# Reordered copies in a four-layer attention and expert kernel: a copy ahead of a normalisation, output spreading on VectorE, half-word reads of rounded values

## The reference

```python
x = x + L0_xattn(ln(x), ctx)   # 8 heads of 64: softmax(q k' / 8) v, projection, bias
x = x + L0_ffn(ln(x))          # 16 heads of 64 with rope and causal mask, then 31 experts of which 3 count, one shared
x = x + L1_xattn(ln(x), ctx)   # 16 heads of 8, key mask
x = x + L1_ffn(ln(x))          # 16 heads of 8 on 4 key heads, rope, causal; then 8 gated experts of which 2 count
x = x + L2_xattn(ln(x), ctx)   # linear in x plus a mean over ctx
x = x + L2_ffn(ln(x))          # 32 gated experts of which 4 count, with a capacity
x = x + L3_xattn(ln(x), ctx)   # one head of 128, two kinds of position
x = x + L3_ffn(ln(x))          # the quantised gated layer below
# L3_ffn, with act_qdq(t) = clip(round(t / s), -32768, 32767) * s,  s = max(|t|) / 32767 over the whole tensor
x = act_qdq(x)
up = act_qdq(x @ dequant(w_up).T)
gate = act_qdq(x @ dequant(w_gate).T)
sig = clip(round(sigmoid(gate) * 65536), 0, 65535) / 65536
gate = act_qdq(gate * sig)
o = act_qdq(gate * up)
return o @ dequant(w_down).T
```

## Time and profile before

| what | value |
|---|---|
| runs (3) | median 1324.61 us, 1323.27 to 1331.30 |
| profiled execution, own time | 1321.66 us |
| its span, first to last instruction | 1319.8 us, mean granted TensorE clock 0.961 |
| busy: PE / PEld / DVE / ACT / POOL | 88% / 68% / 75% / 66% / 42% |
| chain that ended last, by engine | PE 59%, ACT 17%, DVE 14%, issue 7% |
| steps of l0x, without POOL beside them | 7.97 us |
| steps of l0f | 14.54 us |
| steps of l1x | 8.18 us |
| steps of l1f | 8.34 us |
| l3m, from the end of DVE's first scale of the gate (1252.94) to the join of the six maxima (1284.87) | 31.9 us |

### The profile page before, as it was taken

The page is one execution under the profiler, slowest core; times in us unless marked ns, Lnnn a source line. Parts: engine busy times, 40 slices in busy tenths (PEclk is TensorE's granted clock), DMA queues, the critical chain, the costliest instruction groups (busy, mean ns, idle before and its releaser), DMA issues.

```text
span 1319.8 us, 29320 instructions
## 1 busy us (share of the span) xinstructions
PE 1160.2 (88%) x10082; PEld 894.7 (68%) x10082; DVE 995.9 (75%) x2234; ACT 875.7 (66%) x2403; POOL 560.5 (42%) x670
## 2 busy tenths in 40 slices
PE   7889889999988999997888899988999989997815
PEld 4677777788766788885666677766788666666403
DVE  6676677667758899997777766767666787887787
ACT  4666466656654799995888777764566447775684
POOL 5710366766653222255222231132877417881100
PEclk8999999999998999997999999998999899998967
DMA  5230000000002556650000010003222028750001
GB/s 168 60 93 16 20 2 2 2 3 2 2 2 87 181 210 212 209 208 1 2 2 2 3 42 2 2 2 114 88 88 84 0 55 206 190 139 1 1 0 33
DMA packets 38865, 83.71 MB, mean 63 GB/s; under 512 B 6066, under 2 KB 19762, under 8 KB 38740
## 3 DMA queue, kind: packets, MB, share of 16 engines
q1 hardware_dynamic: 38740, 82.07, 20.2%
HBM read 80.40 MB, written 1.64 MB: 62 GB/s over the span
## 4 chain that ended last, share of the span: by engine, by line
PE 59%; ACT 17%; DVE 14%; issue 7%; POOL 2%; DMA 1%; ACTq 0%; SPq 0%; POOLq 0%; DVEq 0%
PE score_bank L1662 18%; ACT h_all L1096 13%; PE f_bank L1696 6%; PE score_bank L1521 6%; PE f_bank L1422 4%; PE turn_bank L1537 4%; PE turn_bank L1696 3%; PE out_bank L1696 3%; PE out_bank L1577 2%; PE out_bank L1546 2%; DVE top_score L2006 2%; PE f_bank L1447 1%; DVE work L2018 1%; PE f_bank L1454 1%; DVE part_max L2404 1%
## 5 line engine op out<-in xcount | busy, mean ns | idle before, releaser
L1096 ACT ACTIVATE h_all<-score_bank,top_score 128x128 f32<-128x128 f32 x896 | 276.6, 400 | 101.3 <-DVE top_score L2006 101.2
L1662 PE MATMUL score_bank<-parts 128*128 128x512 f32 x1040 | 296.4, 403 | 9.8 <-DVE h_parts L2212 6.6
L1662 PEld LDWEIGHTS score_bank<-parts 128*128 128x128 f32 x1040 | 191.9, 190 | 75.2 <-DVE h_parts L2212 19.0
L2006 DVE TENSOR_REDUCE top_score<-score_bank 128x4 f32<-128x512 f32 x224 | 143.1, 681 | 105.2 <-PE score_bank L1521 105.2
L2212 DVE TENSOR_TENSOR h_parts<-score_bank,h_parts 128x512 fp32r<-128x512 f32 x260 | 178.3, 686 | 2.7 <-ACT h_parts L1211 2.4
L1211 ACT ACTIVATE h_parts<-score_bank 128x512 fp32r<-128x512 f32 x260 | 155.5, 598 | 31.8 <-PE f_bank L1696 8.5
L778 POOL TENSOR_TENSOR small<-small,half_neg 128x4 f32<-128x4 f32 (+4 forms) x24 | 36.6, 1528 | 177.0 <-DVE small L1981 83.2
L1537 PE MATMUL turn_bank<-CF,h_all 128*128 128x128 f32 x512 | 81.7, 283 | 30.3 <-DVE work L2018 19.0
L1537 PEld LDWEIGHTS turn_bank<-CF,h_all 128*128 128x128 f32 x512 | 56.1, 142 | 57.1 <-POOL h_all L803 18.1
L1188 ACT ACTIVATE score_bank<-score_bank,wset 128x512 f32<-128x512 f32 x128 | 84.6, 662 | 11.8 <-PE score_bank L1662 7.0
L2184 DVE TENSOR_TENSOR score_bank<-work,score_bank 128x512 f32<-128x512 f32 x124 | 86.3, 696 | 8.2 <-ACT score_bank L1188 5.6
(11 more groups left out here) (417 smaller groups left out, 2623.6 us busy)
## 6 DMA issues: line engine op xcount, KB each, us to landing
work<-gates_l0m SPq DMA_DIRECT2D x62, 512.0 KB, 3.9
W0X<-gates_l2m SPq DMA_DIRECT2D x32, 256.0 KB, 3.9
CTX<-gates_l2m SPq DMA_DIRECT2D x32, 256.0 KB, 3.9
wset<-in_l0m SPq DMA_DIRECT2D x32, 128.5 KB, 3.6
W0X<-gates_l1m SPq DMA_DIRECT2D x8, 512.0 KB, 3.8
wset<-in_l1m SPq DMA_DIRECT2D x8, 384.0 KB, 4.6
CTX<-gates_l1m SPq DMA_DIRECT2D x6, 512.0 KB, 4.0
big<-in_w0f SPq DMA_DIRECT2D x4, 512.0 KB, 3.9
```

Source lines behind the costliest of these rows:

```text
L1096: last = act.activation(held[c][:, P * m:P * m + P], score_bank[c][:, P * m:P * m + P], ACT.Exp, bias=top_score[c][:, m:m + 1], **sums)
L1662: last = pe_.matmul(bk[:, :], wt, y[:, x], start=(part == 0), stop=(part == len(parts_of) - 1))
L2006: dve.tensor_reduce(top_score[c][:, :], split(score_bank[c][:, :], HEADS), AX_X, ALU.max, negate=True)\
```

## The change

1. l0x: on DVE, C 0 of the batch before stands ahead of N 0 of the own batch.
2. l1x and l1f: SP is DVE's, behind M 3, with the same waits and the same signal; OB comes behind C 1 on DVE and behind T 1 on PE. In l1x C 2 goes from DVE to ACT, behind OT.
3. The matmul of two columns ahead of the causal mask is dropped (l0f and l1f).
4. l3m: `gate_steps` and `other` are dropped. The sigmoid and the products read the low 16 bits of the rounded float as an int16, with a step of two (`steps_in`). A one-column Sigmoid stands ahead of the wait for the first scale. Copies and chunk maxima come in another order, three of U's roundings after the wait for the third scale, three among the last roundings of the gate.
5. POOL's wait at the first two batches of l1f names the use of the front bank by l1x's own count of fronts (4) rather than l1f's (3).

```diff
@@ -54,4 +55,4 @@
              ("F", 3, "next")],
-        DVE=[("M", 0, "own"), ("M", 1, "own"), ("CS", 0, "next"), ("OP", 0, "before"), ("N", 0, "own"), ("C", 0, "last"), ("C", 1, "last"),
-             ("N", 1, "own"), ("Y", 0, "after")],
+        DVE=[("M", 0, "own"), ("M", 1, "own"), ("CS", 0, "next"), ("OP", 0, "before"), ("C", 0, "last"), ("N", 0, "own"),
+             ("C", 1, "last"), ("N", 1, "own"), ("Y", 0, "after")],
         POOL=[]),
@@ -70,8 +71,8 @@
         PE=[("S", 0, "own"), ("OP", 0, "before"), ("F", 1, "next"), ("V", 0, "last"), ("V", 1, "last"), ("V", 2, "last"),
-            ("V", 3, "last"), ("F", 2, "next"), ("T", 0, "own"), ("OB", 0, "last"), ("T", 1, "own"), ("F", 3, "next"),
+            ("V", 3, "last"), ("F", 2, "next"), ("T", 0, "own"), ("T", 1, "own"), ("OB", 0, "last"), ("F", 3, "next"),
             ("F", 0, "after"), ("T", 2, "own"), ("OT", 0, "last"), ("T", 3, "own")],
-        ACT=[("F", 0, "next"), ("E", 0, "own"), ("SP", 0, "last"), ("E", 1, "own"), ("F", 1, "next"), ("E", 2, "own"),
-             ("E", 3, "own"), ("F", 3, "next"), ("OT", 0, "last"), ("C", 3, "own")],
-        DVE=[("M", 0, "own"), ("OP", 0, "before"), ("M", 1, "own"), ("M", 2, "own"), ("M", 3, "own"), ("F", 2, "next"),
-             ("C", 0, "own"), ("OB", 0, "last"), ("C", 1, "own"), ("C", 2, "own")],
+        ACT=[("F", 0, "next"), ("E", 0, "own"), ("E", 1, "own"), ("F", 1, "next"), ("E", 2, "own"),
+             ("E", 3, "own"), ("F", 3, "next"), ("OT", 0, "last"), ("C", 2, "own"), ("C", 3, "own")],
+        DVE=[("M", 0, "own"), ("OP", 0, "before"), ("M", 1, "own"), ("M", 2, "own"), ("M", 3, "own"), ("SP", 0, "last"), ("F", 2, "next"),
+             ("C", 0, "own"), ("C", 1, "own"), ("OB", 0, "last")],
         POOL=[("Y", 0, "after")]),
@@ -79,8 +80,8 @@
         PE=[("S", 0, "own"), ("OP", 0, "before"), ("F", 1, "next"), ("V", 0, "last"), ("V", 1, "last"), ("V", 2, "last"),
-            ("V", 3, "last"), ("F", 2, "next"), ("T", 0, "own"), ("OB", 0, "last"), ("T", 1, "own"),
+            ("V", 3, "last"), ("F", 2, "next"), ("T", 0, "own"), ("T", 1, "own"), ("OB", 0, "last"),
             ("F", 0, "after"), ("T", 2, "own"), ("OT", 0, "last"), ("T", 3, "own")],
-        ACT=[("F", 0, "next"), ("E", 0, "own"), ("SP", 0, "last"), ("E", 1, "own"), ("E", 2, "own"), ("E", 3, "own"),
+        ACT=[("F", 0, "next"), ("E", 0, "own"), ("E", 1, "own"), ("E", 2, "own"), ("E", 3, "own"),
              ("C", 2, "own"), ("OT", 0, "last"), ("C", 3, "own")],
-        DVE=[("M", 0, "own"), ("OP", 0, "before"), ("M", 1, "own"), ("M", 2, "own"), ("M", 3, "own"), ("F", 1, "next"),
-             ("C", 0, "own"), ("OB", 0, "last"), ("F", 2, "next"), ("C", 1, "own")],
+        DVE=[("M", 0, "own"), ("OP", 0, "before"), ("M", 1, "own"), ("M", 2, "own"), ("M", 3, "own"), ("SP", 0, "last"), ("F", 1, "next"),
+             ("C", 0, "own"), ("C", 1, "own"), ("OB", 0, "last"), ("F", 2, "next")],
         POOL=[("Y", 0, "after")]),
@@ -328,2 +328,7 @@
 
+        def steps_in(t, at):
+
+            h = HIDDEN_ORDER[at]
+            return t[:, 1024 * h:1024 * h + 1024].bitcast(I16).rearrange("p (n two) -> p n two", two=2)[:, :, 0]
+
 
@@ -823,3 +828,3 @@
 
-                                r, k = place(front_at["l1x"], L["front"], PAIRS - 1, s, 0)
+                                r, k = place(front_at["l1x"], LAYERS[2]["front"], PAIRS - 1, s, 0)
                                 pool.wait_ge(f_drained[r], k + 1)
@@ -1104,7 +1108,2 @@
                             .then_inc(copied if L["dim"] == 64 else copied_by["ACT"], 1)
-                    if what == "SP":
-
-                        act.wait_ge(weighed, unit_no(L, i, s, 0) + 8)
-                        act.wait_ge(regrouped, narrow_no(L, i, s) + 1)
-                        act.activation(spread_o[:, :], out_bank[:, :], ACT.Copy).then_inc(gathered, 1)
                     if what == "OT":
@@ -1334,2 +1333,4 @@
 
+            act.activation(prob_rec[0][:, 0:1], top_score[0][:, 0:1], ACT.Sigmoid)
+
             act.wait_ge(step("l3m.scale"), 1)
@@ -1358,11 +1359,6 @@
             def sigmoid(at):
-                act.wait_ge(step("l3m.g"), at + 1)
+                act.wait_ge(step("l3m.g_round"), at + 1)
                 if at >= 2:
                     act.wait_ge(step("l3m.gs"), at - 1)
-                act.activation(sig[at % 2][:, :], piece(big, at), ACT.Sigmoid, scale=quant[:, 2, 2:3]).then_inc(step("l3m.sig"), 1)
-
-            def other(at):
-
-                act.wait_ge(step("l3m.u_round"), at + 1)
-                act.activation(piece(U, at), piece(U, at), ACT.Identity, bias=less_magic[:, :]).then_inc(step("l3m.u"), 1)
+                act.activation(sig[at % 2][:, :], steps_in(big, at), ACT.Sigmoid, scale=quant[:, 2, 2:3]).then_inc(step("l3m.sig"), 1)
 
@@ -1374,13 +1370,8 @@
                 rounded(big, at, 2, "l3m.g_round")
-                if at < 3:
-                    copies(0, at + 1)
-                if at == 4:
-                    act.wait_ge(step("l3m.scale"), 3)
-                if at >= 4:
-                    rounded(U, at - 4, 1, "l3m.u_round")
+                if 0 < at < 4:
+                    copies(0, at)
                 sigmoid(at)
-            for at in range(2, 6):
+            act.wait_ge(step("l3m.scale"), 3)
+            for at in range(3):
                 rounded(U, at, 1, "l3m.u_round")
-            for at in range(2):
-                other(at)
             act.wait_ge(step("l3m.scale"), 4)
@@ -1388,4 +1379,4 @@
                 rounded(big, at, 3, "l3m.round3")
-                if 1 <= at <= 4:
-                    other(at + 1)
+                if at < 3:
+                    rounded(U, at + 3, 1, "l3m.u_round")
             act.wait_ge(step("l3m.scale"), 5)
@@ -1497,4 +1488,2 @@
 
-                            pe_.matmul(banks[0][:, 0:2], ident_bf, own_bf[:, 0:2], start=True, stop=True, skip_group_check=True)
-
                             for j in range(4):
@@ -2019,2 +2008,7 @@
                             .then_inc(copied if L["dim"] == 64 else copied_by["DVE"], 1)
+                    if what == "SP":
+
+                        dve.wait_ge(weighed, unit_no(L, i, s, 0) + 8)
+                        dve.wait_ge(regrouped, narrow_no(L, i, s) + 1)
+                        dve.tensor_copy(spread_o[:, :], out_bank[:, :]).then_inc(gathered, 1)
                     if what == "OB":
@@ -2465,6 +2459,2 @@
 
-            def gate_steps(at):
-                dve.wait_ge(step("l3m.g_round"), at + 1)
-                dve.tensor_scalar(piece(big, at), piece(big, at), MAGIC, None, ALU.subtract).then_inc(step("l3m.g"), 1)
-
             def by_sigmoid(at):
@@ -2474,3 +2464,3 @@
                 link(dve.tensor_scalar(sg, sg, 65535.0 / 65536.0, MAGIC / 65536.0, ALU.min, ALU.add))
-                dve.scalar_tensor_tensor(piece(big, at), sg, MAGIC / 65536.0, piece(big, at), ALU.subtract, ALU.mult)\
+                dve.scalar_tensor_tensor(piece(big, at), sg, MAGIC / 65536.0, steps_in(big, at), ALU.subtract, ALU.mult)\
                     .then_inc(step("l3m.gs"), 1)
@@ -2484,13 +2474,9 @@
             chunk_max(0, 0)
-            gate_steps(0)
-            chunk_max(0, 1)
             for at in range(6):
-                if at < 5:
-                    gate_steps(at + 1)
                 last = by_sigmoid(at)
-                if at < 2:
-                    others = chunk_max(0, at + 2)
-                if at == 1:
-                    join_max(others, 1, slice(0, 12))
+                if at < 3:
+                    others = chunk_max(0, at + 1)
                 if at == 2:
+                    join_max(others, 1, slice(0, 12))
+                if at == 3:
                     scale(1, 2)
@@ -2502,4 +2488,4 @@
                 dve.wait_ge(step("l3m.round3"), at + 1)
-                dve.wait_ge(step("l3m.u"), at + 1)
-                dve.scalar_tensor_tensor(piece(big, at), piece(big, at), MAGIC, piece(work, at), ALU.subtract, ALU.mult)\
+                dve.wait_ge(step("l3m.u_round"), at + 1)
+                dve.scalar_tensor_tensor(piece(big, at), piece(big, at), MAGIC, steps_in(work, at), ALU.subtract, ALU.mult)\
                     .then_inc(step("l3m.p"), 1)
```

More of the change, by code:

```diff
@@ L15 @@
 U8 = mybir.dt.uint8
+I16 = mybir.dt.int16
 P = 128
@@ L269, in build @@
         quant = sb("quant", [P, 6, 4])
-        less_magic = sb("less_magic", [P, 1])
         part_max = sb("part_max", [P, 24])
@@ L895, in _ @@
             pool.memset(ones_row[:, :], 1.0)
-            pool.memset(less_magic[:, :], -MAGIC)
             for s in range(2):
@@ L2484, in _ @@
             chunk_max(0, 0)
-            gate_steps(0)
-            chunk_max(0, 1)
             for at in range(6):
-                if at < 5:
-                    gate_steps(at + 1)
                 last = by_sigmoid(at)
-                if at < 2:
-                    others = chunk_max(0, at + 2)
-                if at == 1:
+                if at < 3:
+                    others = chunk_max(0, at + 1)
```

(3 more changed lines are left out.)

## The result

| kernel | median of its runs, us | ratio to before, 95% interval |
|---|---|---|
| before | 1324.01 (1319.62 to 1331.30, 20 runs) | |
| changed | 1332.88 (1325.63 to 1338.52, 20 runs) | 1.0062 (1.0047 to 1.0077) |

The changed kernel is 8.9 us slower, 0.62%: within the 1% that the prediction gave 0.80, and 1.9 us above its 1331.0 (its sum had +6.4). The profiled execution took 1338.52, with a span of 1336.7 against 1319.8.

The account below looks back on a forecast made before the run. No engine is full, so stages were bound separately: ACT sets l1x, OB takes its place; DVE bounds l3m. +12.0 + 2.4 - 1.6 - 1.4 - 5.0 = +6.4 gave 1328.1 profiled, 1331.0 predicted; range 1319 to 1341.

Parts of the forecast that it names:

- Part 1: l1x: OB ends 7.47 after S, then OT and C2 delay S; step 9.0, +12.0 us (+2.5 to +14).
- rival B: l1x: OB binds but S doesn't wait for C2; +0.17 a step, total -3.1, 1321.5 us; chance 0.14.
- the clock's fall in l1x: l1x: sign that the prediction is wrong, if the granted clock falls there, where PE's gaps get longer.
- Part 2: l1f: OB ends 7.64 after the masks' start, step 8.50 against 8.34; +0.16 a step, +2.4 us.
- Part 3: l0f: dropping the small matmul saves 0.1 in each of 16 steps, -1.6 us; l1f counted elsewhere.
- The end 0: l0f, small matmul: bound with no saving, as the masks' first load then shows the same 0.1.
- Part 4: l0x: C0 ahead of N0 gains only where POOL holds DVE up, steady step 0; -1.4 us (0 to -2).
- Part 5: l3m: six gate steps and DVE idle go, 0.9 new idle, table load hidden; -5.0 us.
- Rival C: l3m: strided 16-bit reads cost VectorE double, 12 x 1.22 = +14.6, 1345.6 us; chance 0.07.
- Rival D: l3m: the table is loaded a second time before the first sigmoid, +1.3, 1332.3 us; chance 0.03.
- its end of 8.35: l1x: lower bound of the step, if C2 didn't hold S (OB, OT, T3, S alone).
- Rivals A: l1x, l1f: OB doesn't bind and SP's leaving ACT pays; total -30.8, 1293.8 us; chance 0.10.

Follow-up runs that it names:

- C2 ahead: Changed kernel with ACT's C2 ahead of OT in l1x, nothing else: 1319.16 us, ratio 0.9954 to the kernel before.
- SP ahead of M3: "C2 ahead" with DVE's SP ahead of M3, OB ahead of C0 and C1, both layers: 1306.29 us, ratio 0.9859 to the kernel before.
- C2 back on DVE: "C2 ahead" with OB ahead of C1 (DVE) and T1 (PE) in l1x and l1f, plus l1x's C2 on DVE behind C1: l1x steps 8.39 to 8.40.

## Why the prediction was right, and where not

The parts are numbered as in the prediction.

**Part 1, l1x: right, in mechanism and size.** OB's end was put at 7.47 behind S and is there; the step at 9.0 and is 8.98. Two smaller terms cancel: C2 ends at 8.66, not 8.85, and from there to S it takes 0.33 to 0.36, not 0.15. "C2 ahead" shows that C2 behind OT was worth 0.79 of the step and the rest of the new order, OB's later place and SP's leaving together, only 0.02 (8.20 against 8.18), where rival B had 0.17; that is the double count told under part 2. The 0.33 could have been read before: S waited for C2 already, then on DVE and over at 689.69, and began at 690.02:

```profile
689.00 0.69 DVE L2018 COPY work<-score_bank 128x512 f32<-128x512 f32 x1 [0.29 <-PE score_bank L1537]
```

The stage as a whole, first S to the masks of l1f, grew by 15.5 us (147.5 against 132.0), where 12 were said; it grew by 13.0 and 13.6 in the two other profiles with this order. What goes beyond 12 is put down to the granted clock (last section), which the prediction priced at nothing although it gave the clock's fall in l1x as a sign of being wrong. That sign came. The loop of waits stood, and the term for the clock was missing.

**Part 2, l1f: right place, size off.** OB ends 7.63 behind the masks (7.64 said). But from there to the masks it takes 0.75 and not 0.86: OT starts 0.06 behind OB's end, where I added 0.07 for the signal and 0.11 for the way to the matmul, two names for one gap. +0.04 a step, +0.6 in 15, not +2.4.

**Part 3, the small matmul: the step that failed is "it lies in PE's own line", so that its 0.1 would be saved.** The end 0 was the truth in l0f: the first 32-row piece has a gap of about 0.1 ahead of it, and the small matmul lay in that gap. In l1f its 0.08 was real in the order before, and the new order took it away. The Trainium skill (TensorEngine Tiling (Array Packing), Key Properties) says that a change of the tiling mode drains TensorE; the 0.1 that stays in l0f may be what one sees of it, and I had read the 0.09 of the earlier trace rows as leaving no room for it. No run here shows the drain by itself.

**Part 4, l0x: right where it looked, and it did not look at the join.** The step with the cast gained 1.0 (0.9 said) where the cast meets N0, and the steady step nothing. The join's 0.65, a wait for T0 placed in front of the next layer's rope products, was missed: what is queued behind a waiting instruction must be read at the last step too, where the queue behind is another one. The sum is near 0, not -1.4. The Trainium skill (SBUF — State Buffer, Who interferes with whom) has the later of VectorE and GpSimd wait for the other where both need the port pair that they share. The trace agrees for N0 and for y_tok, which took 2.38 here as well; the copy out of PSUM beside the same cast took its usual 0.69.

**Part 5, l3m: right.** -5.2 against -5.0: idle 0.84 for 0.9, join 26.7 for 27. Rival C is out: the strided 16-bit reads cost VectorE nothing (1225 and 1218 ns). ScalarE pays 17 ns (1161 for 1144). The Trainium skill (VectorE: DVE Perf Modes, Mode 1×) has one result a cycle with odd strides too, so no price on VectorE, and the trace agrees. Rival D is out: no second load.

**The sum.** By its steps: +12.0 + 0.6 + 0 + 0 - 5.2 = +7.4, and 1.0 to 3.5 of clock in l1x (15.5, 13.0 and 13.6 less 12.0); the medians say +8.9. That +6.4 came so near is in part luck: l1f was 1.8 too high and l3m 0.2, the small matmul 1.6, l0x 1.4 and the clock 1.0 to 3.5 too low, and these cancel in part. Two slips of addition in the prediction change nothing: its end of 8.35 adds up to 8.33, and its own upper ends to 1338, not 1336. Rivals A and B fell: A's promise, that SP's leaving frees ACT, is seen only once OB and C2 stand so that nobody waits long for them: 0.45 a step in l1x and 0.46 in l1f with SP ahead of M3.

## What to carry to other kernels

When work goes from one engine's line to another's, follow the new line to the last thing that somebody waits for, and ask of each item what stands ahead of it: here 0.6 us moved off ScalarE was lost because OB slid behind it, and because C2, a copy that the next S needs, was put behind OT, which waits for OB. Ask the same at the joins between stages, where another queue stands behind the same item. An instruction seen in front of a gap may lie in a gap that stays when it is gone; look whether a wait or the gap ends last there.

## What the runs showed of the hardware

**The granted clock falls in l1x only with the longest steps.** The stretch 640 to 740 us (columns: busy us and count of PE, PEld, DVE, ACT, POOL, then the granted clock, DMA share, GB/s), of before, the changed kernel, "C2 ahead" and "C2 back on DVE":

```profile
640.00:740.00 100.00, 83.75 (x1207) 65.73 (x1211) 73.88 (x165) 80.83 (x281) 31.07 (x72) 1.00 0.01 2
```
```profile
640.00:740.00 100.00, 78.55 (x1073) 64.03 (x1077) 64.69 (x142) 72.96 (x253) 24.37 (x65) 0.93 0.01 2
```
```profile
640.00:740.00 100.00, 82.56 (x1197) 66.06 (x1195) 73.70 (x169) 82.22 (x283) 31.01 (x72) 1.00 0.01 2
```
```profile
640.00:740.00 100.00, 76.55 (x1188) 65.34 (x1188) 78.59 (x176) 74.25 (x262) 27.80 (x66) 1.00 0.01 2
```

All three profiles with steps of 8.98 have 0.93 here, that is, some stretches at 1.2 GHz among 2.4; all nine others (steps 7.73 to 8.40) have 1.00. What sets it is open. In each step of the changed kernel PE waits 0.8 for tmpT and 0.7 for ACT's copy. "C2 ahead" has the first of these waits and 1.00. "C2 back on DVE" has two waits as long (0.79 for SP's copy, 0.73 for C2), less busy time of PE, and 1.00 too, so the length of the waits alone does not explain it. Steps in which the clock fell are up to 9.8 long. It costs 1.0 to 3.5 us, an estimate from the three stages' lengths, and is in the change's account.

**Another stretch differs from run to run, whatever the kernel**, 380 to 400 us, here the changed kernel (0.67; the kernel before has 0.91 with the same busy time of PE, 13.97):

```profile
380.00:400.00 20.00, 13.96 (x161) 11.20 (x145) 8.44 (x30) 8.98 (x38) 6.79 (x6) 0.67 0.00 1
```

Four profiles of twelve have 0.61 to 0.67 there, and the way from the last masks of l0f to the first S of l1x takes them 240.0 to 240.4 us; six have 0.91 and take 235.6 to 236.1; two have 1.00 and take 233.4 and 234.4. The kernel with l3m alone is among the slow ones, the one with items 2 and 5 alone is not. This is 4.7 of the 16.9 us between the two profiled executions and a share of the spread between single runs of one kernel. What sets it was not tried.
